# Macaron block (MoE feed-forward, selective scan, MoE feed-forward): routing weights taken off TensorE and VectorE, multiplied in on GpSimd, with a reordered pipeline

## The reference

```python
x = x + 0.5 * ffn(layernorm(x))
x = x + mamba(layernorm(x))
x = x + 0.5 * ffn(layernorm(x))

def ffn(xf):                                   # 8 experts of width 176, top 2, and a shared one of width 352
    top_logits, idx = top_k(xf @ Wg, 2)
    w = zeros((n, 8)).at[rows, idx].add(softmax(top_logits))
    h = silu(einsum('tc,ech->eth', xf, W1)) * einsum('tc,ech->eth', xf, W2)
    y = einsum('eth,ehc,te->tc', h, W3, w)     # each hidden value times its expert's routing weight
    return y + (silu(xf @ Ws1) * (xf @ Ws2)) @ Ws3

def mamba(x):                                  # d_inner 256, 16 states, 4 taps
    x_in, z = split(x @ W_in + b_in)
    xc = silu(causal_conv(x_in)); B, C = split(xc @ W_xp + b_xp); delta = softplus(xc @ W_dt + b_dt)
    h[t] = exp(delta * A) * h[t-1] + delta * xc * B[t];  y[t] = sum over the states of h[t] * C[t]
    return layernorm_alpha_beta(x + ((y + D * xc) * silu(z)) @ W_out + b_out)
```

## Time and profile before

| | us |
|---|---|
| median of 3 runs | 2434.92 (2432.38 to 2435.53) |
| the profiled execution, its own time | 2431.15 |
| its span, first to last instruction | 2429.2 |
| PE busy, share of the span | 1814.9 (75%) |
| DVE busy | 1877.2 (77%) |
| ACT busy | 1315.8 (54%) |
| POOL busy | 1071.5 (44%) |
| mean granted clock of TensorE | 0.896 |

### The profile page before, as it was taken

The page is one execution under the profiler, slowest core; times in us unless marked ns, Lnnn a source line. Parts: engine busy times, 40 slices in busy tenths (PEclk is TensorE's granted clock), DMA queues, the critical chain, the costliest instruction groups (busy, mean ns, idle before and its releaser), DMA issues. The chain is left out here.

```text
span 2429.2 us, 21997 instructions
## 1 busy us (share of the span) xinstructions
PE 1814.9 (75%) x4768; PEld 789.5 (32%) x4768; DVE 1877.2 (77%) x3077; ACT 1315.8 (54%) x1927; POOL 1071.5 (44%) x939
## 2 busy tenths in 40 slices
PE   4775787777778777788778777787877877785457
PEld 2332333333333333333333333333333333332123
DVE  2488878888887878887887888878878887887753
ACT  1465565555556555656556565655565655564422
POOL 3045635436263453635345363543636354363631
PEclk9695999899998999989989899989899999998688
DMA  2034323433343434334343433333434334344340
GB/s 76 18 80 111 93 65 94 99 84 92 73 101 73 105 78 104 78 79 102 80 98 85 96 87 79 91 91 79 104 87 94 70 87 104 74 104 100 87 91 5
DMA packets 62124, 206.45 MB, mean 85 GB/s; under 512 B 7648, under 2 KB 28864, under 8 KB 47680
## 3 DMA queue, kind: packets, MB, share of 16 engines
q0 software_dynamic: 18432, 125.84, 26.1%
q1 hardware_dynamic: 35840, 76.03, 9.6%
q10 hardware_dynamic: 7744, 3.57, 0.6%
HBM read 74.87 MB, written 4.72 MB: 33 GB/s over the span
## 5 line engine op out<-in xcount | busy, mean ns | idle before, releaser
L479 POOL TENSOR_TENSOR prod<-hist,crow 128x1024 f32<-128x1024 f32 x224 | 528.9, 2361 | 763.4 <-DVE hist L770 763.4
L770 DVE TENSOR_TENSOR_SCAN hist<-decay,dbx 128x1024 f32<-128x1024 f32 x256 | 625.0, 2441 | 24.6 <-ACT decay L569 21.1
L961 PE MATMUL ps_y<-gated,down_w 128*128 128x512 f32 (+1 forms) x896 | 497.8, 639 | 11.2 <-DVE gated L779 10.9
L569 ACT ACTIVATE decay<-delta,a_neg 128x510 f32<-128x510 f32 x512 | 326.6, 708 | 1.5
L733 DVE TENSOR_TENSOR dbx<-du,ps_bc 128x1024 f32<-128x1024 f32 x256 | 310.8, 1214 | 3.5 <-PE ps_bc L923 0.7
L589 ACT ACTIVATE silu<-ps_h1a 128x512 f32<-128x512 f32 (+1 forms) x224 | 132.8, 593 | 251.5 <-PE ps_h1a L951 247.3
L939 PE MATMUL ps_wb<-wT,sel_w 96*128 96x512 bf16 x352 | 138.9, 395 | 170.0 <-DVE gated L779 166.9
L951 PE MATMUL ps_h1b<-xnT,up_w 128*128 128x512 f32 x448 | 257.1, 658 | 10.8 <-ACT silu L589 10.7
L951 PE MATMUL ps_h1a<-xnT,up_w 128*128 128x512 f32 (+1 forms) x448 | 256.0, 655 | 12.0 <-ACT xnT L594 12.0
L923 PE MATMUL ps_bc<-bT,sel_b 96*128 96x512 bf16 x256 | 112.7, 440 | 200.8 <-DVE dbx L733 199.9
L966 PE MATMUL ps_h2a<-xnT,up_w 128*128 128x512 f32 (+1 forms) x448 | 253.5, 650 | 0.0
(11 more groups left out here) (136 smaller groups left out, 2327.6 us busy)
## 6 DMA issues: line engine op xcount, KB each, us to landing
yacc<-prod POOLq DMA_DIRECT2D x112, 1024.0 KB, 8.1
crow<-c_rows SPq DMA_DIRECT2D x128, 512.0 KB, 3.9
yacc<-yacc POOLq DMA_DIRECT2D x16, 512.0 KB, 4.5
xres<-L_attn_x SPq DMA_DIRECT2D x16, 256.0 KB, 7.0
out<-xres SPq DMA_DIRECT2D x16, 256.0 KB, 2.3
up_w<-L_ffn_W ACTq DMA_DIRECT2D x2, 704.0 KB, 5.9
down_w<-L_ffn_W ACTq DMA_DIRECT2D x1, 704.0 KB, 6.9
c_rows<-cT SPq DMA_DIRECT2D x16, 32.0 KB, 4.6
```

The lines of the kernel that those rows point to most:

```text
L479: nc.gpsimd.tensor_tensor(prod[:, (pair - 1 + odd) % 2, s % 2, :, :], hist[:, s % 2, :, :], c_all, ALU.mult).then_inc(prod_done, 1)
L569: ins = nc.scalar.activation(decay[:, s % NA, half, :, 1:LEN], d[:, :, 1:LEN], ACT.Exp, scale=a_neg[:, half, s:s + 1])
L770: nc.vector.tensor_tensor_scan(hist[:, s % 2, :, :].rearrange("p h t -> p (h t)"), decay[:, s % NA, :, :, :].rearrange("p h b t -> p (h b ...
L961: nc.tensor.matmul(ps_y[:], down_w[0:rd, jd, :], gated[0:rd, (posd + NCHUNK * f_parity(k, fd)) % NSILU, :], start=(posd == 0), stop=(posd ...
```

## The change

**The weights.** The matmul L939, the tile `ps_wb`, the selection matrix `sel_w`, the five-instruction split and the second multiply on DVE (L779) go. The weights stay float32 (`wtok`), are transposed once (`wT`, 8 rows), stored to DRAM by the SP queue (`w_rows`), and for each expert's chunk read back by two transfers of the SP queue that spread the rows of the one or two experts that the chunk covers over its 128 partitions (`wrow`, a ring of `NW` = 4). POOL multiplies the chunk by it, in place. The chunk lives in one ring of seven buffers, `act_h`, from Silu to the down-projection, which PE now does three slots behind (`BACK` = 3) instead of two. `ps_h2` comes free at DVE's only multiply, which stands ahead of the scan in an even slot.

**The pipeline.** `PLAN` is written anew: the second feed-forward of group k-2 now runs in slots 0 to 13, the first one of group k+2 in slots 15 to 28. Two more bodies are thus partly filled at either end (-2 to 17 instead of -2 to 16), and bodies 0, 1, 14 and 15 have one feed-forward where full bodies have two; the full ones are 2 to 13 (before: 1 to 14). The folding DMA of `yacc` moves from slot 1 to slot 3, `gate_y` from 3 to 5. The SP queue gets a plan of its own.

```diff
 PLAN = {
-        3: ["gate_y"], 4: ["outproj", "stats0"], 5: ["x1n", "outT"], 6: ["resid"], 7: ["stats3"],
-        9: ["ln_norm"], 10: ["norm0"], 12: ["stats1"], 13: ["norm1"], 14: ["xT1"], 15: ["logits1", "xT0"],
-        16: ["route1", "yT0", "addy0"], 17: ["stats2", "weights1"], 18: ["norm2", "wT1", "logits0"],
-        19: ["route0", "xT2"], 20: ["in0"], 21: ["in1", "conv0a"], 22: ["in2", "conv0b", "conv1a"],
-        23: ["in3", "conv1b"], 24: ["dt0", "weights0"], 25: ["dt1"], 26: ["xproj", "bparts"],
-        27: ["cT"], 28: ["delta", "bT"], 29: ["wT0"], 31: ["yT1", "addy1"],
+        0: ["x1n", "stats0"], 1: ["stats2"], 2: ["norm0"], 3: ["xT0", "norm2", "fold"], 4: ["logits0"],
+        5: ["route0", "xT2", "gate_y"], 6: ["outproj", "in0"], 7: ["weights0", "in1", "conv0a"], 8: ["wT0", "outT"],
+        9: ["resid", "in2", "conv0b"], 10: ["in3", "stats3", "conv1a"], 12: ["conv1b", "ln_norm"], 14: ["dt0"],
+        15: ["dt1"], 17: ["yT1", "addy1", "stats1"], 18: ["norm1", "xproj"], 19: ["bparts"], 20: ["xT1"],
+        21: ["logits1"], 22: ["route1", "cT"], 23: ["bT"], 24: ["weights1"], 25: ["delta"], 26: ["wT1"],
+        31: ["yT0", "addy0"],
     }
-    UP0, UP1 = 0, 15
+    UP1, UP0, BACK = 0, 15, 3
+
+    SP_PLAN = {
+        0: ["c1"], 3: ["c2", "w1:4"], 5: ["w1:5"], 6: ["w1:6", "c3", "w1:7"], 8: ["w1:8", "store_w0"], 9: ["w1:9"],
+        10: ["w1:10", "c4"], 11: ["w0:0"], 12: ["w0:1"], 13: ["w0:2"], 14: ["w0:3", "c5"], 17: ["store_x"],
+        19: ["c6", "w0:4"], 20: ["w0:5"], 21: ["w0:6", "w0:7", "c7"], 23: ["w0:8"], 24: ["w0:9"], 25: ["w0:10"],
+        26: ["store_w1", "w1:0", "next_c0"], 27: ["w1:1"], 28: ["w1:2"], 29: ["w1:3"],
+    }
...
+            def rows_w(k, odd, f, e, route=None):
+
+                place, value = w_turn(k, odd, f, e)
+                n = fcount(k, f, ECHUNK, e)
+                if not isinstance(n, int) or n >= NW:
+                    sp.wait_ge(weighted, n - NW + 1)
+                if e == 0:
+                    sp.wait_ge(w_stored, 16 * (route + 1))
...
+                for lo, hi, row in ((0, cut, first), (cut, P, last_row)):
+                    sp.dma_start(wrow[lo:hi, place, :], w_rows[f, row, :].partition_broadcast(hi - lo)
+                                 ).then_inc(w_ready[place], 16)
...
                 for slot in range(SLOTS):
+                    d = gate_unit(k, slot)
+                    if d is not None and ORDER[d[1]] < ECHUNK:
+                        f, pos = d
+                        place, value = w_turn(k, odd, f, ORDER[pos])
+                        pool.wait_ge(h2_taken, fcount(k, f, NCHUNK, pos + 1))
+                        pool.wait_ge(w_ready[place], value)
+                        nc.gpsimd.tensor_tensor(act_h[:, pos % NACT, :], act_h[:, pos % NACT, :], wrow[:, place, :],
+                                                ALU.mult).then_inc(weighted, 1)
...
                         act.wait_ge(h1_full, n + 1)
-                        if not isinstance(n, int) or n >= NSILU:
-                            act.wait_ge(gate_done, n - NSILU + 1)
+                        if not isinstance(n, int) or n >= NACT:
+                            act.wait_ge(down_done, n - NACT + 1)
...
-                        if j >= ECHUNK:
-                            if not isinstance(n, int) or n >= NSILU:
-                                dve.wait_ge(down_done, n - NSILU + 1)
-                            nc.vector.tensor_tensor(gated[0:r, place, :], silu[0:r, place, :], ps_h2[pos % 2][0:r, :],
-                                                    ALU.mult).then_inc(gate_done, 1)
-                        else:
-                            nc.vector.tensor_tensor(silu[:, place, :], silu[:, place, :], ps_h2[pos % 2][:], ALU.mult
-                                                    ).then_inc(mid_done, 1)
+                        nc.vector.tensor_tensor(act_h[0:r, pos % NACT, :], act_h[0:r, pos % NACT, :],
+                                                ps_h2[pos % 2][0:r, :], ALU.mult).then_inc(h2_taken, 1)
...
-                    if d is not None and j < ECHUNK:
-                        dve.wait_ge(mid_done, fcount(k, f, ECHUNK, pos - (NCHUNK - ECHUNK) + 1))
-                        dve.wait_ge(wb_full, fcount(k, f, ECHUNK, pos - (NCHUNK - ECHUNK) + 1))
...
-                        nc.vector.tensor_tensor(gated[:, place, :], silu[:, place, :], ps_wb[:], ALU.mult
-                                                ).then_inc(gate_done, 1)
...
-                            pe.wait_ge(gate_done, n - 1)
+                            pe.wait_ge(h2_taken, n - 1)
```

255 lines of the change are left out of this document (140 added, 115 removed).

## The result

The changed kernel takes 2595.34 us (median of 4 runs, 2591.96 to 2604.90) against 2433.65 for the kernel before on the same chip: ratio 1.0673, 95% interval 1.0639 to 1.0706. Forecast was 2330, with a range up to 2425. The sign is wrong and the time lies outside the range.

What follows compares the result with a forecast made beforehand. The kernel was paced by waits between DVE and PE; afterwards the path shared by scans and POOL would be the floor. 707 us of fill, drain and partly filled bodies plus 12 x 135 gave 2327, forecast 2330 us; range 2237 to 2425.

Steps and rivals of the forecast that it cites:

- 117.4 + 17.5 = 135 us a body: Full body: 117.4 us of shared-path use plus 17.5 us in which that path lies idle, 8 less than now.
- shared path: Scans and POOL instructions exclude each other, the second waiting for the whole other; 117.4 us a full body, its new floor.
- idle term: Full body: 5 us around POOL's accumulations, 6 for feed-forward sums, 6.5 for the body's turn, statistics powers and routing.
- this wait at 3: DVE standing in line for a feed-forward's sums (yT, addy), 3.19 us today; two a body, 6 us together.
- The down-projection hardly ever waiting for POOL: Expected sign in the profile after: PE's down-projection would hardly ever wait for POOL's multiply.
- The down-projection a slot later costs nothing while the ring of seven holds: Transfers part: three slots of distance instead of two cost 0 while seven chunk buffers suffice.
- slower: POOL's serial rate: Rival: POOL falls two slots behind and its in-order work sets the body at 147 us, 2471 + 4; chance 0.13.
- my sign of being wrong: PE waiting for POOL's multiply in most slots, POOL waiting for wrow, or a scan's start hanging on the product two states back.
- what I held against this rival: Against POOL's serial rate: descriptor work (8 x 0.93 us) and powers can lie beside a scan.
- term of 27.7: Shared path of a full body: 22 new POOL multiplies of 1.26 us each add 27.7 us.
- Taken away: Full body: 14.8 us of L779 off DVE, 8.7 of L939 off PE, leaving DVE about 102 and PE 104.
- Fill, drain, transfers: Fill 153 us, drain 111; row transfers hidden, 16 us available against 3.9, or 4.6 + 3.9 behind the store.

Runs made afterwards that it cites:

- e2: Changed kernel without POOL's multiply and the row transfers, routing weights left out: 2350.8 us.
- e8: New plan with transfers, multiply on DVE behind the scan, and the decays of states 10 and 11 moved from slot 16 to 15: 2414.8 us.
- e12: e8 with the decays of states 8 and 9 also moved from slot 12 to 13, computation complete: 2393.4 us.
- e7: Changed kernel with POOL's multiply by a constant tile of ones and no row loads, routing weights left out: 2592.4 us.
- e10: e2 plus full-size POOL multiplies between constant tiles, for which the down-projection doesn't wait: 2468.5 us.
- e14: Changed kernel with POOL's multiply cut to one column, down-projection four slots behind and second feed-forward one slot earlier: 2391.6 us.
- e11: Changed kernel with the down-projection four slots behind instead of three and the second feed-forward one slot earlier: 2481.4 us.
- e9: Changed kernel with PE's matmul of ps_h2 ahead of the down-projection in a slot, not behind it: 2590.4 us.
- e6: Old plan with the change's ring of seven and three-slot distance, but no weighting at all: 2409.2 us.

## Why the prediction was wrong

**The step that failed first** reads "On top come stretches in which the path lies idle ... So 117.4 + 17.5 = 135 us a body". The shared path was taken for the floor of a body, with 17.5 us of idle time on top. e2 has no multiply on it, so by the same sum its path holds 117.4 - 27.7 = 89.7 us, and its full body takes 136.6: 46.9 us of idle path, not 17.5. Even with PE's 104 us as the floor in its place, which PE kept in e2 (103.0), the same idle term gives 121.5, 15 too few. The new plan is held elsewhere. The two longest distances between neighbouring scans in the full bodies of e2 are 16.4 us (slots 16 to 18) and 14.4 (12 to 14); the next is 10.5. In the first DVE waits 3.66 us for a Silu behind the softplus (at 1011.09) and 5.86 (at 1018.77) for the sum out of a feed-forward (addy1), whose transpose PE can make only when ACT has copied `yT`, and that copy stands behind a burst. I had priced this wait at 3. In the second, normalisation, table load, burst and table load stand ahead of a Silu. Here are ACT's rows in the changed kernel and then DVE, which waited 6.38 us for it:

```profile
1545.54 1.63 ACT L624 ACTIVATE rtok<-rtok,nbiasr,stdr 128x128 f32<-128x128 f32 x4
1547.19 1.28 ACT L637 ACT_TABLE_LOAD   x1
1548.49 2.55 ACT L637 ACTIVATE decay<-delta,a_neg 128x510 f32<-128x510 f32 x4
1551.06 1.28 ACT L657 ACT_TABLE_LOAD   x1
1552.35 0.60 ACT L657 ACTIVATE act_h<-ps_h1b 128x512 f32<-128x512 f32 x1
```

```profile
1552.98 0.69 DVE L820 TENSOR_TENSOR act_h<-act_h,ps_h2b 128x512 f32<-128x512 f32 x1 [6.38 <-ACT act_h L657]
```

e8 and e12 confirm by experiment that ACT holds these two pairs: two entries of a table took 58 us off, in part by fewer table loads. I had listed the decays at the turn of a body only, and had priced no ACT queue in the slots that the plan fills anew.

**"The down-projection hardly ever waiting for POOL"** failed next, and cost as much as the multiply itself: 124 us by e7 less e10, and 135 by what the fourth slot takes off. The same step stands in the part on the transfers: "The down-projection a slot later costs nothing while the ring of seven holds". The multiply of a chunk is asked for in the next slot, but in POOL's order it stands behind the product of the slot before, that product behind its scan, and each of them once more behind whatever holds the path. Where POOL has small steps besides, three slots are not enough, and four are (e14: 1.1 us of wait). How one such wait travels can be read in a full body of the changed kernel, POOL first, then PE, ACT and DVE:

```profile
1554.83 4.48 POOL L505 TENSOR_TENSOR act_h<-act_h,wrow 128x512 f32<-128x512 f32 x2
```

```profile
1549.34 1.02 PE L1012 MATMUL ps_y<-act_h,down_w 128*128 128x512 f32 x2
...
1558.14 2.08 PE L1012 MATMUL ps_y<-act_h,down_w 128*128 128x512 f32 x2 [5.20 <-POOL act_h L505]
...
1560.01 1.91 PE L1017 MATMUL ps_h2a<-xnT,up_w 128*128 128x512 f32 x2
1561.72 2.41 PE L1059 MATMUL ps_m<-xconv,w_dt 128*128 128x512 f32 x4
```

```profile
1564.16 0.69 ACT L730 ACTIVATE dtmp<-ps_m,b_dt_c 128x512 f32<-128x512 f32 x1 [9.57 <-PE ps_m L1059]
...
1565.45 1.28 ACT L736 ACT_TABLE_LOAD   x1
...
1571.48 0.60 ACT L657 ACTIVATE act_h<-ps_h1b 128x512 f32<-128x512 f32 x1
```

```profile
1562.03 0.69 DVE L820 TENSOR_TENSOR act_h<-act_h,ps_h2a 128x512 f32<-128x512 f32 x1 [3.68 <-PE ps_h2a L1017]
...
1572.11 0.69 DVE L820 TENSOR_TENSOR act_h<-act_h,ps_h2b 128x512 f32<-128x512 f32 x1 [7.19 <-ACT act_h L657]
```

POOL came late to its two multiplies: ahead of them stood the three instructions of ln_norm (from 1548.12 to 1552.56) and a product. Then a scan held the first until 1557.03 (1553.59 + 3.44). PE waited 5.20 us, and behind the wait two matmuls of the down-projection took 2.08 us, where two of them had taken 1.02 at 1549.34. The mean granted clock was 1.00 from 1549 to 1553, 0.60 from 1558 to 1564 and 1.00 again to 1566.4: for most of that stretch PE ran at the lower of the two levels of its clock (1.2 and 2.4 GHz). From 1558.14 to its end at 1564.13 the work up to dt1 took 5.99 us, and the same matmuls 3.60 in e11. The projection for delta (dt1) came out late; ACT had waited 9.57 us for it, then ran the whole softplus with its table loads ahead of the next Silu, and DVE stood 7.19 us. The same ACT rows in e11, where dt1 was not late:

```profile
1492.91 0.69 ACT L730 ACTIVATE dtmp<-ps_m,b_dt_c 128x512 f32<-128x512 f32 x1 [2.52 <-PE ps_m L1059]
```

It waited 2.52 us. In the twelve full bodies this wait is 4.9 to 9.7 us in the changed kernel, 7.9 to 9.0 in e9, and 2.5 in e11. That speaks for why e9 didn't help: the matmuls of the slot behind the wait, not `ps_h2` alone, are what the others need. The rival "slower: POOL's serial rate" named this wait and the side, but had its price by another rule (POOL never without work, 147 us). POOL was without work: 265.2 us ahead of L505 alone, and e11 has the same work in bodies of 145.2. Nor did my sign of being wrong come out as I put it, PE waiting in most slots: four waits a body were enough. Of what I held against this rival, descriptor work does lie beside a scan (25 of 128 in the kernel before, at 0.9 us), but the powers don't: nine that began beside a scan took 3.08 us, 1.0 elsewhere. The rows 1289.36 and 1291.20 showed how late POOL gets in its own queue; a slot-by-slot count of POOL against the distance of three slots would have shown it, and I did not make one.

**The length of the multiply** was right alone (1.27 us, forecast 1.26), and a multiply that nobody waits for costs 118 us (e10), 7.9 a full body (144.5 less 136.6), where its own time on the path is 27.7. So the term of 27.7 was too large as an addition to a body, and the idle term too small by more. The Trainium skill ("SBUF — State Buffer", Who interferes with whom) calls the shared port pair an exclusive lock. The trace agrees: the scan kept its 2.28 us, and the multiply beside it ended 1.07 us behind the scan's end. That a scan also loses to four POOL instructions one behind the other (7.25 us) is more than the whole of one other instruction, by which I had priced a meeting.

**"Taken away"**: DVE was counted rightly, 101.5 us in a full body of e2 for a forecast of 102. But 202 us came back in the whole kernel as standing time (1648.5 to 1850.8). PE was counted at the clock of before, 104 us. It kept that in e2 (103.0 at 0.92) and not with the multiply: 107.2 at 0.89 in e10, 110.5 at 0.86 in the changed kernel, for the same matmuls. So both costs, of the multiply and of the wait, hold a part that is the lower clock; how much of each was not separated. And e6 gains only 1% in the old order without any weighting: the 166.9 us of PE's wait for DVE did not turn into time, be it that slack had collected there or that the clock took it.

**Fill, drain, transfers.** 154.1 for 153, 107.8 for 111, and rows that land in 3 to 4 us. Bodies 0, 1, 14 and 15 were forecast 13.5, 16.8, 7.9 and 4.0 us too low; whether by the cause of the full ones was not tried. The lower end of the range, 2237, is 3 us above its own sum (707 + 12 x 127 = 2231, and 3 as for the forecast), which changes nothing.

The whole account, in medians: before 2434; new plan and no weighting 2351; the multiply in POOL's queue +118; the down-projection's wait +124; the transfers +3, within the noise; after 2595. The two moves of ACT's bursts were not tried in the old plan, so whether e12's gain needs the new one is open.
